# A graph network with attention and experts on one core: weights prepared in the first block, and the division of the second edge stage moved to DVE

## What is computed

```python
xn = layernorm(x)
x  = x + gat(relu(gat(xn, W1, ...)), W2, ...) + mix(xn, Wqkv, Wout, bout)
x  = x + moe(layernorm(x))            # 16 experts, 2 for each node

def gat(x, src, dst, W, a_src, a_dst, b):            # 4 heads of 64
    h = x @ W
    e = leaky_relu((h . a_src)[src] + (h . a_dst)[dst])
    ex = exp(e - segment_max(e, dst)[dst])
    s = segment_sum(ex, dst)
    return segment_sum(h[src] * (ex / s[dst]), dst) + b
```

## Time and profile before

| | |
|---|---|
| median of 3 runs | 3288.85 us (3284.75 to 3294.06) |
| the profiled execution | 3300.46 us |
| its span, first to last instruction | 3298.8 us |
| PE, DVE, ACT, POOL busy | 65%, 55%, 28%, 59% |
| gathers (L931), both layers | 1568, busy 1581.8 us |
| mean granted TensorE clock | 0.819 |

### The profile page before, as it was taken

One profiled execution on the slowest core, in us unless ns is written; L12 is line 12 of the kernel. 1 busy time (PEld: TensorE's weight loads), 2 busy tenths in 40 slices (PEclk: granted clock), 3 DMA queues, 4 the chain that ended last, 5 costly groups with the idle time before them and its releaser, 6 DMA issues. The chain is left out here.

```text
span 3298.8 us, 50988 instructions
## 1 busy us (share of the span) xinstructions
PE 2148.4 (65%) x10263; PEld 1637.1 (50%) x10264; DVE 1829.2 (55%) x4382; ACT 931.4 (28%) x2254; POOL 1932.8 (59%) x1918
## 2 busy tenths in 40 slices
PE   0636666566667676645566665666666556999996
PEld 0424444344434454433444444444445445999994
DVE  4655555565555565564455554655555456555555
ACT  0412222222322223220122221222222123444445
POOL 0246666666666666617666666666666621666663
PEclk9967888788888788876777777777777767999998
DMA  2634444444444444425445454454454425555555
GB/s 55 190 107 117 116 121 118 117 116 124 116 120 122 116 122 119 114 93 147 126 130 139 127 137 124 132 136 127 128 135 128 126 69 155 102 101 105 102 97 168
DMA packets 273930, 399.38 MB, mean 121 GB/s; under 512 B 90593, under 2 KB 187256, under 8 KB 273850
## 3 DMA queue, kind: packets, MB, share of 16 engines
q0 software_dynamic: 101728, 251.76, 31.2%
q1 hardware_dynamic: 131417, 104.31, 11.7%
q10 hardware_dynamic: 40720, 42.61, 3.9%
HBM read 344.28 MB, written 54.62 MB: 121 GB/s over the span
## 5 line engine op out<-in xcount | busy, mean ns | idle before, releaser
L931 POOL DMA_INDIRECT gathered<-table,idx x1568 | 1581.8, 1009 | 830.3 <-issue 464.1
L1215 PE MATMUL psA_e<-gathered,hotf 128*128 128x260 f32 x3136 | 892.7, 445 | 109.9 <-issue 55.4
L1215 PEld LDWEIGHTS psA_e<-gathered,hotf 128*128 128x128 f32 x3136 | 706.8, 229 | 269.0 <-issue 131.7
L1112 ACT ACTIVATE gathered<-t_e 128x32 f32<-128x32 f32 x196 | 45.1, 230 | 1106.0 <-issue 603.8
L1003 DVE SCALAR_TENSOR_TENSOR acc<-psA_e,lower,acc 128x260 f32 x196 | 95.8, 489 | 284.1 <-issue 227.3
L1626 POOL DMA_INDIRECT moe_d<-xscaled,xtarget x113 | 179.2, 1586 | 124.7 <-DVE xtarget L1570 46.9
L988 DVE TENSOR_TENSOR hotf<-iota,code_r 128x1024 f32<-128x1024 bf16 x196 | 240.3, 1226 | 7.9 <-issue 7.9
L995 DVE TENSOR_TENSOR gathered<-gathered,psW_e 128x2048 f32<-128x2048 f32 x98 | 223.5, 2280 | 2.3 <-issue 2.3
L1598 PEld LDWEIGHTS xpsH<-xxT,w1e 128*128 128x128 f32 x1808 | 220.5, 193 | 6.2 <-ACT xxT L1527 0.4
L995 DVE TENSOR_TENSOR gathered<-gathered,psDW_e 128x2048 f32<-128x2048 f32 x98 | 223.4, 2279 | 0.0
L1607 PE MATMUL xpsO<-w,hidT 128*128 x904 | 217.4, 383 | 7.3 <-DVE hidT L1559 6.5
(11 more groups left out here) (314 smaller groups left out, 3252.3 us busy)
## 6 DMA issues: line engine op xcount, KB each, us to landing
codes<-codes_d SPq DMA_DIRECT2D x196, 256.0 KB
gathered<-table,idx POOLq DMA_INDIRECT x1568
w<-in_L_ffn_w ACTq DMA_DIRECT2D x8, 2048.0 KB
xb<-in_L_ffn_b SPq DMA_DIRECT2D x113, 128.0 KB
w<-xnT_d SPq DMA_DIRECT2D x98, 128.0 KB
table<-acc POOLq DMA_DIRECT2D x49, 130.0 KB, 2.7
table<-acc ACTq DMA_DIRECT2D x49, 130.0 KB
xnT_d<-xnT ACTq DMA_DIRECT2D x49, 128.0 KB, 1.8
```

The source lines that it names most:

```text
L931: pool.indirect_dma_start(out=G[:, q, k, :], out_offset=None, in_=table, in_offset=bass.IndirectOffsetOnAxis(ap=idx[:, q, k:k + 1], axis=0 ...
L1215: ins = pe.matmul(psA[:, q, 0:GW], hotf[:, q, k, :], G[:, q, k, :], start=(k == 0), stop=(k == KT - 1))
```

## The change

It has four edits.

1. The first block of `project_inputs` (loads, attention columns, transposes, means) goes into `prepare_edges`, now `prepare`. The loads are started on ACT's queue, at the start of the kernel. DVE does the weights' work before it waits for the edge lists, and PE turns the weights before it turns the chunks' ends.
2. In the second edge stage DVE computes `hidden` itself, right behind the reciprocal: for each head acc times the reciprocal plus x, as one scalar_tensor_tensor of 128x64. ACT's `divide` and PE's matmul of x through the identity are gone there. The first edge stage keeps `divide` on ACT.
3. `load_x` of the second edge stage runs at offset 4 in place of 6.
4. ACT waits for one load of codes and the third load of indices before it starts the experts' weights.

```diff
 # edit 1: prepare(), the former prepare_edges(); the first block of project_inputs() is gone
+            weights = Chain(dve, s["w_steps"])
+            dve.memset(acc[:, NT:NT + 2, :], 0.0)
...
+            dve.wait_ge(s["w_loaded"], 144)
+            attention_columns(dve, weights, wext, att, attw)
+            attention_columns(dve, weights, wext1, att1, attw)
+            for g in range(6):
+                dve.wait_ge(s["w_turned"], g + 1)
...
             dve.wait_ge(s["loaded"], 64)
...
+        @block.scalar
+        def _(act):
+            act.dma_start(wext[:, :, 0:C], a["L0_gnn_W1"].rearrange("(k p) n -> p k n", p=P)).then_inc(s["w_loaded"], 16)
...
             pe.wait_ge(s["consts"], 1)
+            pe.wait_ge(s["w_loaded"], 144)
+            for g in range(6):
...
             pe.wait_ge(s["tiled"], 1)
 # edit 2: gat_edges(), second layer
-                dve.wait_ge(s["hidden"], t + 1)
                 if attention:
+                    dve.wait_ge(s["hidden"], t + 1)
                     dve.wait_ge(s["out"], t * 2 + 2)
...
                 dve.reciprocal(rden[:], acc[:, ds(d, 1), C:GW].rearrange("p o h -> p (o h)")).then_inc(s["rden"], 1)
+                if not attention:
+                    dve.wait_ge(s["rden"], t + 1)
+                    dve.wait_ge(s["mixed"], t + SLOTS)
+                    dve.wait_ge(s[f"x_in{b}"], 32 * use + 32)
+                    for h in range(H):
+                        ins = dve.scalar_tensor_tensor(hidden[:, h * CH:(h + 1) * CH], acc[:, ds(d, 1), h * CH:(h + 1) * CH].rearrange("p o f -> p (o f)"),
+                                                       rden[:, h:h + 1], x[b][:, h * CH:(h + 1) * CH], ALU.mult, ALU.add)
+                    ins.then_inc(s["hidden"], 1)
...
-                    pe.matmul(psY[:, 0:C], ident[:], x[b], start=False, stop=False)
 # edit 3
-                rounds = chunks(sp, new_pass(sp), nothing, (0, load), (-1, load_codes), (6, load_x, True))
+                rounds = chunks(sp, new_pass(sp), nothing, (0, load), (-1, load_codes), (4, load_x, True))
 # edit 4
+                act.wait_ge(s["codes_in1"], 16)
+                act.wait_ge(s["idx_in2"], 16)
                 for e in range(0, NX - 4, 4):
                     act.dma_start(w1[:, e:e + 4, :, :], a["L0_ffn_w1"][e:e + 4].rearrange("e (k p) f -> p e k f", p=P)).then_inc(weights_in, 16)
```

More of the change, by code:

```diff
@@ L207, in build @@
             edges = (codes_d, partition, iota, acc, own, peak, parts, windows)
-            stage(prepare_edges, a, srcp, codes_d, partition, ident, identb, ones, iota, eps, code, lower, upper, first_tile, passes)
+            attention_weights = (wkvT, wq, woutT, wext1)
             spare = w1[:, 14:16].rearrange("p e k f -> p (e k f)")
@@ L212, in build @@
             combine = (a, xnT_d, xf_d, moe_d, ident, ones, eps, mixM, hot, extra, w1, weights_in, ahead)
-            stage(project_inputs, a, xnT_d, table[0], ident, eps, acc, dtab, dotsT, wkvT, wq, woutT, wext1)
+            with ExitStack() as first:
+                wext0 = sb("wext0", [P, 2, HW], F32, first)
+                stage(prepare, a, srcp, codes_d, partition, ident, identb, ones, iota, eps, code, lower, upper, first_tile, passes,
+                      acc, dtab, dotsT, wext0, attention_weights)
+                stage(project_inputs, a, xnT_d, table[0], ident, eps, acc, dtab, wext0)
             stage(bounds, 0, ident, ones, acc, dtab, own, peak, parts, wide)
@@ L360, in _ @@
             pe.wait_ge(s["consts"], 1)
+            pe.wait_ge(s["w_loaded"], 144)
+            for g in range(6):
+                if g:
+                    pe.wait_ge(s["w_moved"], g)
+                for j in range(4):
+                    if g < 4:
+                        kc, q = g // 2, g % 2
+                        ins = pe.transpose(psW[:, j * P:(j + 1) * P], wkv[:, 4 * q + j, kc * P:(kc + 1) * P], ident[:])
+                    else:
+                        ins = pe.transpose(psW[:, j * P:(j + 1) * P], wout[:, g - 4, j * P:(j + 1) * P], ident[:])
+                ins.then_inc(s["w_turned"], 1)
             pe.wait_ge(s["tiled"], 1)
@@ L462, in _ @@
             tiles(sp, (0, load))
-        @block2.gpsimd
+        @block.gpsimd
         def _(pool):
@@ L470, in _ @@
             pool.wait_ge(s["h_stored"], 16 * NT)
-        @block2.vector
+        @block.vector
         def _(dve):
@@ L490, in _ @@
             tiles(dve, (1, normalise), (0, stats))
-        @block2.scalar
+        @block.scalar
         def _(act):
@@ L515, in _ @@
                 act.wait_ge(s[f"xT_out{q}"], 16 * uses(q))
-        @block2.tensor
+        @block.tensor
         def _(pe):
@@ L1113, in exps, with divide @@
                 act.activation(psW[:, 0:KT * H].rearrange("p (k h) -> p k h", h=H), t[:], ACT.Exp).then_inc(s["weights"], 1)
-            def divide(t, i, b, use):
-                d = dest_of(act, i)
-                act.wait_ge(s["rden"], t + 1)
-                if not attention:
-                    act.wait_ge(s["yb"], t + 1)
-                act.wait_ge(s["fin_turned" if attention else "mixed"], t + (1 if attention else SLOTS))
-                for h in range(H):
-                    ins = act.activation(hidden[:, h * CH:(h + 1) * CH], acc[:, ds(d, 1), h * CH:(h + 1) * CH].rearrange("p o f -> p (o f)"), ACT.Copy, scale=rden[:, h:h + 1])
-                ins.then_inc(s["hidden"], 1)
-            if attention:
+            if attention:
+                def divide(t, i, b, use):
+                    d = dest_of(act, i)
+                    act.wait_ge(s["rden"], t + 1)
+                    act.wait_ge(s["fin_turned"], t + 1)
+                    for h in range(H):
+                        ins = act.activation(hidden[:, h * CH:(h + 1) * CH], acc[:, ds(d, 1), h * CH:(h + 1) * CH].rearrange("p o f -> p (o f)"), ACT.Copy, scale=rden[:, h:h + 1])
+                    ins.then_inc(s["hidden"], 1)
                 def squares(t, i, b, use):
@@ L1190, in _ @@
                 act.sem_inc(s["gate_logits"], 1)
-                chunks(act, new_dest(act), nothing, (9, store, True), (8, root, True), (1, exps), (13, gates, True), (11, xf_turned, True), (6, divide, True), (8, normalise, True))
+                chunks(act, new_dest(act), nothing, (9, store, True), (8, root, True), (1, exps), (13, gates, True), (11, xf_turned, True), (8, normalise, True))
                 act.wait_ge(s["gap"], 1)
```

101 lines of the change are left out of this document (37 added, 64 removed).

## The result

The changed kernel takes 3265.08 us, the kernel before 3281.4 us (medians of 15 runs each, in rounds on one chip). The ratio is 0.9944, with a 95% interval of 0.9932 to 0.9957, so the change is worth 18 us (14 to 22). The forecast was 22 us (3288.85 to 3267). Its number holds. Its working holds in part only, as the rows of each stretch show.

The account below looks back on a forecast made before the run. POOL's gathers bound the edge loops, after a start chain that nothing overlaps. 3300.46 - 24.1 (start) - 1.5 (experts' loads) - 1 (tail) + 5 (held gathers) = 3278.9 profiled; the median is 11.6 lower, so 3267, own range 3255 to 3279.

Parts of the forecast that it names:

- The rival of late weights: First block: weights stay behind the edge lists, come at 45.8 us, gain only 0.3 us; 3291 us, chance 0.06.
- counterweight: Start of second edge loop: 6 MB beside the first gathers and ACT's 7.49 us of issues cost 0 to 6 us.
- The step of the new operations' own time: Second edge loop: DVE's four operations take about 1.0 us a tile, 49 us in all, covered by POOL's gathers.
- the 5 us of holding: Second edge loop: DVE's new operations with two SBUF inputs hold POOL's gathers; 5 taken, 11 by rule, 38 at worst.
- If POOL can go in between them: Second edge loop: gathers proceed between the four DVE operations, losing at most 0.1 us at a time, some 3 us.
- The tail: End of second edge stage: one pair of PE instructions less, DVE's 1.0 us for ACT's 1.3; -1 us taken.
- DVE's microsecond on the path: Second edge loop, between reciprocal and logits: DVE's added 1.0 us a tile costs 49 us; 3311 us, chance 0.10.
- A part of it shows: Second edge loop: DVE's added time costs up to 17 us; 3279 us, up to 3295, chance 0.09.
- the worst holding of gathers: Second edge loop: worst phase in each tile, DVE's operations hold gathers (0.9 - 0.13) x 49 = 38 us.
- POOL's pause shrinks: Second edge loop: slots released in time, a quarter of the 161.5 us of pauses goes; 3227 us, chance 0.11.
- sign for being right: Second edge loop stays at 1189 us within 10; one of several signs listed.
- sign for being wrong: Second edge loop takes over 1205 us; one of several signs listed.

Follow-up runs that it names:

- One input in SBUF: Changed kernel, but DVE's four operations only multiply, without x as second SBUF input, and PE adds x by matmul again; 2958.39 us, ratio 0.9877 to the kernel before.
- the unread operations: Kernel before with weights first and experts' loads late, division on ACT, plus four DVE operations a tile that nobody reads; 2982.7 us, ratio 0.994 to the kernel before.
- seven divisions: Changed kernel with the four divisions done seven times, 24 unread DVE operations a tile more; 3132.64 us, ratio 1.0439 to the kernel before.

## Why the prediction was right, point by point

**Edit 1, right.** The weights were there at 20.78 (forecast 22, bounds 17.8 and 26.4), their work took 43.75 - 20.78 = 23.0 us (22.9), the list work up to 67.01 another 23.3 (23.3), and the projection's load came at 68.03 (69.3). DVE did not wait for the lists again. The rival of late weights is out. One thing went another way: SP's issue of `dst_i` took 18.05 us, where it had taken 6.55; ACT's nine issues and the weights' transfers ran beside it. It cost nothing, as DVE needed the lists only at 43.75.

**Edit 4, right, but for its counterweight.** The forecast took -1.5: -2.5 for two gathers gained, and +1.0 out of a counterweight of 0 to 6. The table of stretches has -4.9 there, which looks like three times as much. The order of time, the changed kernel:

```profile
1428.39 13.46 DVE L955 TENSOR_TENSOR acc<-acc 128x3136 f32<-128x3136 f32 x4 [0.43 <-ACT acc L1111]
1435.06 1.01 POOL L926 DMA_INDIRECT gathered<-table,idx  x1 [6.84 <-DMA idx<-srcp]
1436.37 2.99 POOL L926 DMA_INDIRECT gathered<-table,idx  x1 [0.30 <-issue]
1439.67 3.00 POOL L926 DMA_INDIRECT gathered<-table,idx  x1 [0.30 <-issue]
1442.97 0.95 POOL L926 DMA_INDIRECT gathered<-table,idx  x1 [0.30 <-issue]
```

The wait before the first gather is 6.84 in place of 11.83 us, 5.0 us less. But two gathers of 3.0 us now stand under DVE's own terms. The gather of 1442.97 starts 14.6 us behind the start of these terms, as that of 1482.16 does in the earlier trace rows; it is the fourth, and that was the second. So two gathers are gained, 2.5 us, just as the forecast had it, and the other 2.5 us come back as longer gathers inside the second loop. The sixteenth gather ends 2.8 us earlier, counted from the start of the own terms. What failed is the counterweight of 1.0: none showed.

**Edit 2, wrong in two sizes and in its sign.** The step of the new operations' own time held on the other chips: they are covered (idle time of POOL unchanged, with four and with eight of them). Each takes 0.281 us, not 0.23, but one starts 0.2 us behind the other, so four take 0.87 us (forecast 0.9). The step that failed is the 5 us of holding. It scaled the row of 2002.40, where a comparison of 1.23 us holds a gather, to operations of a quarter of its length. Under the new ones 18 gathers start in the changed kernel on chip 6 and are 0.1 us longer in all; on the first chip 24, 0.3 us. (The 29 in the expectation of "One input in SBUF" counts a gather twice where two of these operations overlap.) The end that began "If POOL can go in between them" (some 3 us) was the right one, and even that is too much.

What stands in its place is a term that the forecast did not have: edit 2 moves the comparison in the row of gathers. On chip 6 the gathers become 8.2 us shorter with it (792.6 to 784.4, edits 1 and 4 against all four), 6.3 of them under the comparison; on chip 11 6.9 and 5.9 (edit 1 alone against edits 2 and 3). Another 2.0 us of the 10 lie behind the last gather, where the last sum into psY ends 26.0 in place of 28.0 us later. On the first chip the whole change made the gathers 6.2 us longer (787.5 to 793.7), but only 1.7 of these lie under the comparison. 2.5 are the gathers under DVE's own terms (edit 4), and the rest is mostly the usual gather, 0.949 against 0.946 us in these two executions. That the comparison's place is a matter of phase is what the unread operations say: similar work added without taking ACT's away makes 13 us more instead. PE's matmul of x does not set the phase, as the kernel with one input in SBUF has it back and the same gathers. Whether it is ACT's work that is gone or the shorter way to `mixed` stays open.

The Trainium skill, page "SBUF — State Buffer", section "Who interferes with whom", says that a DVE instruction with two SBUF inputs contends with a GpSimd instruction that reads SBUF. The comparison agrees: with one input moved to PSUM its holding went from 34.1 us to 0.7. The same section infers that descriptor generation is spared by `tensor_tensor`; these gathers are not. And the four short operations, with two SBUF inputs, held nothing that counts (0.1 us in all).

**The tail, right in sign.** The forecast took -1. The last sum into psY ends 25.8 us behind the last gather, in place of 28.0: -2.2. The +2.9 of the table's last row comes behind that, in stages whose code is the same.

**Edit 3, right.** The forecast took nothing, and the kernel with x loaded later takes as long as the changed one within the intervals.

**The rivals.** DVE's microsecond on the path (3311) is out: on the other chips the cover is about 2.5 us a tile, 0.87 and 1.6, and the cost seen with seven divisions is what that rival looks like beyond it. On the first chip the loop grew by 12.4 us, not by 49; no run there takes the edits apart. "A part of it shows" (3279) gave a price close to the 12.4 us of the second loop on the first chip, for a reason that the runs do not bear out: half of the 12.4 us are longer gathers, as split above, the other half pauses (idle time in the loop 401.5 before and 407.6 after, without the wait ahead of the first gather). Its upper end of 3295 "with the worst holding of gathers" does not follow from the prediction's own 38 us, which would give 3317. "POOL's pause shrinks" did not come true there either.

**What the number owes to luck.** In the profiles the stretches came to -24.5, -4.9, +12.4 and +2.9, and a first loop that is unchanged gave -14.8 (its pauses 22.5 us shorter, its gathers 7.6 us longer). Without that last term the profiles would differ by 14 us in place of 29. It is not a fixed gain of the change: on the other chips the same loop takes 1056.3 to 1065.6 us behind the old start and 1052.6 to 1066.8 behind the new one. The second loop at 1201.4 us missed the prediction's own sign for being right (1189 within 10) and stayed under its sign for being wrong (1205). On the other chips, where the loops do not pause, the change is worth 36 us, twice the 18 of the first chip. So the close number is in part luck. The prediction said what would make it wrong above all, "a loop whose tile period hangs on the phase between POOL and the other engines". That is what both loops do, and its own range of 3255 to 3279 did not price it.

## What the runs showed of the hardware that was not expected

The first chip and the three others differ by 9% in the same kernel, and all of it lies in the edge loops: 1206.3 and 1189.0 us against 1056.4 and 1029.3. The three others agree within 0.3%. Each chip was used at one time only, so whether this is the chip or its state then is not told apart. On the first chip POOL is idle 414.4 us in the second loop of the changed kernel, on chip 6 245.4. The instructions of the sequencers tell the same. In order of time, the changed kernel on the first chip:

```profile
1914.44 0.70 SPq L909 DMA_DIRECT2D w<-in_x  x1
...
1917.07 0.28 PE L1292 MATMUL psG<-w 128*128 128x16 f32 x1 [1.30 <-issue]
...
1918.65 0.70 SPq L910 DMA_DIRECT2D w<-xnT_d  x1
...
1919.39 0.18 PE L1292 MATMUL psG<-w 128*128 128x16 f32 x1 [2.04 <-issue]
...
1922.58 0.95 POOL L926 DMA_INDIRECT gathered<-table,idx  x1 [3.22 <-remote]
```

and on chip 6:

```profile
1761.82 0.60 PE L1292 MATMUL psG<-w 128*128 128x16 f32 x4
...
1774.14 0.33 SPq L909 DMA_DIRECT2D w<-in_x  x1
...
1774.65 0.33 SPq L910 DMA_DIRECT2D w<-xnT_d  x1
```

An issue of SP takes 0.70 in place of 0.33 us there, and two of the three steps between PE's four small instructions of one `gates` are over 2 us in place of 0.2. Of SP's 290 issues in the second loop 88 take 0.6 us or more in this trace, and 105 of 288 in the kernel before; in each of the twelve traces of the other chips it is two at most. The distances between PE's small instructions are rarer: 4 of 132 are over 0.6 us here, 21 in the kernel before, none elsewhere. POOL's pause of 3.22 us stands behind one of them. That would explain why the pauses of the earlier trace rows cannot be put down to any wait, and why POOL went on so long after the sum that it needed. It is argued from the records, not shown by a run, and what slows the sequencers on that chip is open: none of the variants ran on it. It follows that the account of the second loop above holds for the other chips; on the first one the loop's pauses stay unexplained.

PE's granted clock fell in the second loop with the change, 0.76 to 0.73 of full speed on the first chip and, with the division moved, 0.78 to 0.75 on chip 6 (a mean of stretches at 1.2 and at 2.4 GHz). On chip 6 PE was busy for 705.3 us with 2970 instructions where it had been 709.2 with 3062, although the 92 matmuls of x had taken 46: most of that was spent by the others, which became slower (`add` 463 ns in place of 446). It cost nothing, as POOL's idle time is the same in both.

## What to carry to other kernels

Where one engine's own row is the bound, ask not only whether new work on another engine is covered, but which of that engine's operations can hold the bounding one, and whether the new work moves them. Such a phase was worth -10 to +13 us of a loop of 1030 us here, so it belongs in the range and not in the sum, or it is removed at the root: here one operand moved to PSUM brings 37 us on top of the changed kernel, as much as the whole change (36) on those chips. A pause that no wait explains should be looked at on a second chip before anything is built on it.
